# Two-layer transformer kernel: where the attention's folded maxima are transposed and added within a round

## The reference

```
b, n, c = x.shape                      # 8, 256, 128
qkv = x @ qkv_w.T + qkv_b              # 16 heads of 8 columns
attn = softmax(einsum('bhqd,bhkd->bhqk', q, k) / sqrt(8))
out = einsum('bhqk,bhkd->bhqd', attn, v)
return out @ proj_w.T + proj_b
```

## Time and profile before

| what | value |
|---|---|
| executions | 856.55, 856.58, 864.62 us; median 856.58 us |
| profiled execution | 864.53 us, of which the span from first to last instruction is 862.7 us |
| busy over the span | PE 689.3 us (80%), PEld 540.5 us (63%), DVE 673.7 us (78%), ACT 492.5 us (57%), POOL 128.6 us (15%) |
| granted TensorE clock over the span | mean 0.854 of full speed |
| rounds 0 and 1 of the attention | 24.35 and 20.79 us, clock 0.62 and 0.70 |
| rounds 2 and 3 | 18.80 and 18.77 us, clock 1.00 |
| rounds 4, 5, 6 | 20.45, 20.37, 21.37 us, clock 0.92, 0.92, 0.87 |
| round 7 | 23.14 us, clock 0.65 |
| round 8 | 20.46 us, clock 0.58 |

### The profile page before, as it was taken

One profiled execution on the slowest core, in us unless ns is written; L12 is line 12 of the kernel. 1 busy time (PEld: TensorE's weight loads), 2 busy tenths in 40 slices (PEclk: granted clock), 3 DMA queues, 4 the chain that ended last, 5 costly groups with the idle time before them and its releaser, 6 DMA issues. The chain is left out here.

```text
span 862.7 us, 14707 instructions
## 1 busy us (share of the span) xinstructions
PE 689.3 (80%) x5386; PEld 540.5 (63%) x5386; DVE 673.7 (78%) x1432; ACT 492.5 (57%) x893; POOL 128.6 (15%) x101
## 2 busy tenths in 40 slices
PE   6365765764669879999999867877877889999996
PEld 5254665664557657787778644444444458888886
DVE  3999899999975797989979848788775337777765
ACT  4667577778465566766867633666654543333232
POOL 1112113133304670010000047000000000000000
PEclk9578787777786998999989965899887579999999
DMA  7453343444415301103012040000000000000000
GB/s 230 99 143 111 105 117 99 101 126 121 132 41 179 98 25 55 44 1 99 1 34 66 0 147 0 2 1 2 1 2 1 1 1 1 1 13 1 13 13 13
DMA packets 76699, 48.30 MB, mean 56 GB/s; under 512 B 54994, under 2 KB 64980, under 8 KB 76628
## 3 DMA queue, kind: packets, MB, share of 16 engines
q1 hardware_dynamic: 73268, 44.75, 17.9%
q10 hardware_dynamic: 3360, 2.62, 1.0%
HBM read 37.85 MB, written 9.50 MB: 55 GB/s over the span
## 5 line engine op out<-in xcount | busy, mean ns | idle before, releaser
L983 ACT ACTIVATE hT<-hps,b1s 128x512 f32<-128x512 f32 x128 | 88.0, 691 | 67.3 <-PE hps L897 64.5
L1148 DVE TENSOR_TENSOR hl<-hT,hh 128x512 fp32r<-128x512 f32 x128 | 96.8, 777 | 28.7 <-ACT hh L989 27.2
L1592 DVE TENSOR_REDUCE mx<-s_ps 128x2 f32<-128x512 f32 x128 | 82.5, 687 | 42.0 <-PE s_ps L1351 41.6
L1525 ACT ACTIVATE pt<-st_ps 128x512 f32<-128x512 f32 x128 | 69.7, 600 | 48.4 <-PE st_ps L1361 48.3
L1820 ACT ACTIVATE act_h<-up 128x512 f32<-128x512 f32 x64 | 38.2, 598 | 87.7 <-PE up L1774 87.7
L320 ACT ACTIVATE rest<-rest,par 128x264 f32<-128x264 f32 x128 | 53.7, 502 | 36.7 <-DVE rest L591 36.7
L313 ACT ACTIVATE tap<-cst_s,par 128x328 f32<-128x328 f32 x128 | 72.4, 653 | 3.8 <-DVE par L644 3.8
L1902 DVE TENSOR_TENSOR hid<-act_h,up 128x512 f32<-128x512 f32 x64 | 43.3, 685 | 26.5 <-ACT act_h L1820 13.3
L1785 PEld LDWEIGHTS eo<-wc,hid 128*128 128x128 f32 x512 | 61.7, 192 | 2.4
L1785 PE MATMUL eo<-wc,hid 128*128 128x128 f32 x512 | 62.1, 275 | 0.0
L897 PE MATMUL hps<-xnh,w1h 128*128 128x512 f32 x128 | 55.9, 437 | 5.2 <-POOL w2l L805 4.5
(11 more groups left out here) (340 smaller groups left out, 1699.5 us busy)
## 6 DMA issues: line engine op xcount, KB each, us to landing
kd<-kst SPq DMA_DIRECT2D x16, 512.0 KB, 2.6
xc<-in_x_coarse SPq DMA_DIRECT2D x16, 512.0 KB, 4.2
wdB<-wdd SPq DMA_DIRECT2D x32, 256.0 KB, 5.2
dW<-kd SPq DMA_DIRECT2D x16, 256.0 KB, 3.3
Ks<-kd SPq DMA_DIRECT2D x64, 33.0 KB, 2.1
dW<-kd SPq DMA_DIRECT2D x64, 32.0 KB, 2.1
w1r<-in_w ACTq DMA_DIRECT2D x5, 256.0 KB, 2.9
w2r<-in_w ACTq DMA_DIRECT2D x5, 256.0 KB, 3.4
```

What stands on the lines that cost most here:

```text
L983: nc.scalar.activation(hT[k][:], hps[:, k, :], ACT.Gelu, bias=b1s[:, m:m + 1]).then_inc(h_done, 1)
L1148: nc.vector.tensor_tensor(hl[s % 2][:, k, :], hT[k][:], hh[s % 2][:, k, :].bitcast(F32), ALU.subtract).then_inc(hl_done, 1)
L1525: nc.scalar.activation(pt[h % 8][:].rearrange("p t q -> p (t q)"), st_ps[k][:], ACT.Exp, scale=SCALE)\
L1592: nc.vector.tensor_reduce(mx[:, :, h:h + 1], s_ps[k][:].rearrange("p (t k) -> p t k", t=2), AX, ALU.max).then_inc(s_used, 1)
```

## The change

The order of calls is changed in two places on TensorE and in one on VectorE. No instruction is added or taken away, and no wait is added: each `maxima` takes the waits along that stood before it.

```
@@ TensorE, round i @@
                     project(4 * i + 6)
+                if i - 1 in whole:
+                    pe.wait_ge(proj_used, min(4 * i + 6, PROJ))
+                    maxima(i - 1, 1, 2)
                 scores(i, 1)
...
                 values(i - 1, 0)
-                if i - 1 in whole:
-                    pe.wait_ge(proj_used, min(4 * i + 6, PROJ))
-                    maxima(i - 1, 1, 2)
                 scores(i, 3)
...
                     project(4 * i + 8)
+                scores(i, 5)
+                values(i - 1, 1)
                 if i in whole:
                     if i >= 2:
                         pe.wait_ge(o_ready, 2 * (i - 2) + 1)
                     else:
                         pe.wait_ge(proj_used, 4 * i + 7)
                     maxima(i, 0, 0)
-                scores(i, 5)
-                values(i - 1, 1)
@@ VectorE, round i @@
                 split(4 * i + 6)
+                add_maxima(i - 1, 1, 2)
                 largest(i, 2)
                 split(4 * i + 7)
                 largest(i, 3)
-                add_maxima(i - 1, 1, 2)
```

## The result

The changed kernel takes 851.79 us (median of 12 executions, 848.00 to 854.83) against 859.93 us of the kernel before (12 executions, 854.36 to 864.62). The ratio is 0.9887, with a 95% interval of 0.9862 to 0.9911: about 1.1% faster. The quotient of the two medians alone is 0.9905, so the gain is about 1% by either. The three executions that stood before the prediction had a median of 856.58; with twelve it is 3.4 us higher. The profiled execution of the changed kernel is one of its fastest, 848.22 us, where that of before, 864.53 us, lay above eleven of the twelve, so the two traces lie 16.3 us apart and the medians 8.1 us. The stages are therefore compared round by round.

The account below looks back on a forecast made before the run. In the attention, VectorE's reductions between scores were taken to bound each step at 1.9 us. From the median of 856.58 us, 2.95 for the order and 1.1 for the clock came off: 852.5 us, range 846.5 to 861.

Parts of the forecast that it names:

- The cycle of scores and reductions: Attention rounds: scores start only after VectorE reduced the step before, so a step costs 1.9 us at the least.
- Step 1 and the transposes' price: Round 3: four transposes now stand between a projection and these scores, cost 0.62 us and delay them that much.
- Steps 3 and 4: Round 3: the earlier addition delays the former by 0.88 us; the latter loses its stall but comes 0.10 us later.
- Step 5: Round 3: these scores, no longer behind the transposes and the wait for `averaged`, come 1.06 us earlier.
- Step 6: Round 3: TensorE's own work, 2.69 us with the transposes, sets these scores; the round is 0.45 us shorter.
- The sum at an unchanged clock: Attention stage: 2.25 us less in rounds 2 to 6, with rounds 0, 1 and 7 2.95 us less.
- The clock: Rounds 4 to 6: falls of the granted clock become rarer, worth 4.4 us, of which 1.1 count against the median.
- the third rival: Whole kernel: the clock gives all of its loss back, 849.2 us or 846; chance 0.15.
- The rule on transposes: TensorE: the skill says transposes do not count as work for the full clock, which speaks against the change.
- The rival that rested on it: Rounds 2 to 6: the clock falls more often, about 1.64 us each, 861.8 us in all; chance 0.12.
- the one that nothing is gained: Whole kernel: handoffs from VectorE are the long ones, or round 1 loses; 856.6 us, chance 0.15.
- the one of the full 17.4 us: Attention: both stalls go, 9.3 and 8.1 us, and nothing takes their place; 839.2 us, chance 0.05.

Follow-up runs that it names:

- e5: Changed kernel with the transposes of a batch's first half done twice into the same bank; 849.27 us, ratio 0.9885 to the kernel before.
- e6: Changed kernel with the second half's transposes directly behind a round's first scores, their addition between the first two steps' reductions; 851.03 us, ratio 0.9900.
- e1: Kernel before with only the first half's move, transposes and addition of the maxima earlier; 860.11 us against 860.17, ratio 0.9967.
- e11: Kernel before, order kept, with the repeated work of e3 and the unread matmuls of e9; 848.10 us, ratio 0.9867.
- e9: Changed kernel with added matmuls whose result nobody reads in rounds 6 to 8; 839.43 us, ratio 0.9735 to the kernel before.
- e2: Kernel before with only the second half's move, transposes behind the scores of Step 5 and its values; 852.99 us against 860.17, ratio 0.9923.
- e4: Changed kernel with the addition of the maxima back in its late place, the transposes staying early; 857.03 us, ratio 0.9949 to the kernel before.
- e0: The changed kernel itself, measured again; 849.35 us against 862.06 of the kernel before, ratio 0.9857.
- e3: Kernel before, order kept, with some transposes and projection matmuls done twice inside the two stalls; 856.15 us against 860.17, ratio 0.9952.
- e7: Changed kernel with the transposes of a batch's first half moved behind the scores of Step 6; 845.24 us, ratio 0.9825 to the kernel before.

## Why the prediction was right in the time and short in the size

The time, 852.5 us, was met to 0.7 us, and the range held. The size was not: I forecast 4.1 us less than a median of 856.58, and the medians of twelve lie 8.1 us apart. By the ratio it was faster by 1.1%, and to more than 1% I gave 0.15; by the medians it was 0.95%. That the number fits is luck: the gain was forecast 4.1 us too small, and the median of the three executions of before lay 3.4 us too low, and the two errors nearly cancel.

**The cycle of scores and reductions: right.** Steps that nothing else holds came after 1.92 and 1.85 us, where I had 1.88 and 1.87.

**Step 1 and the transposes' price: too high.** I took 0.62 us for four transposes, from the distance of starts before and behind them. Inserted in unbroken work behind a projection or behind the values they cost 0.44 (step 0 to 1: 2.77 against 2.33; e5: 2.91 against 2.47); directly behind step 0 they cost 0.59 (e6), so the price depends on the neighbours. The old distances, as I read it, held some time that the neighbours take anyway. I used the price twice in a round, and it makes 0.38 of the 0.43 us by which a round beat the forecast.

**Steps 3 and 4: right.** The addition was moved from one overflowing gap to another; e1 shows 0.09 us gained instead of 1.12, where I had 0.10 lost, and the price of the transposes (0.62 for 0.44) makes nearly all of that difference. One of my signs is badly put: what comes later by the addition is the pair of step 2 and then step 3. Step 2 itself came 0.37 later than before (4.70 us behind step 0 instead of 4.33), by the transposes.

**Step 5: right.** 1.85 us against the forecast 1.87.

**Step 6: right in kind.** TensorE's own work sets it (e5); measured 2.48 where I had 2.69.

**The sum at an unchanged clock: the step that was off.** Forecast 2.95 us, measured 7.1 between e11 and e9, of which 6.3 in rounds 2 to 7 at the full clock in both. The terms: rounds 2 to 6 2.25 against 4.4; round 7 0.5 against 1.85; the end of the stage 0 against 0.73; round 1 0.9 against 0.43, at clocks that differ; round 0 a loss of 0.7 against 0.36. In rounds 2 to 6 it is nearly all the price of the transposes, used twice (0.38 of 0.43 us). In round 7 I had priced them at the low clock, at which it ran before. At the full clock and without `project(4i+6)` the round has room for both groups of transposes: steps 0 to 4 take 7.72 us in e9 and 8.51 in e11, steps 4 to 6 3.89 and 4.96.

**The clock: right in direction, uncertain in size.** Falls in rounds 2 to 5 are gone in both profiles of the changed kernel. All profiled executions with a stall left as it was (before, e1, e2, e4) have such a fall, and none of the ten others does (changed, e0, e3 and e5 to e11). With e3, which keeps the order and only fills the stalls, this makes the idle time the cause. Not every stall is followed by a fall (rounds 2 and 3 of before), and what decides stays open. Of the 14.5 us between the two profiled stages, 7.1 are the order by e11 and e9, and the other 7.4, as what is left over, are put down to the clock. Of the 8.1 us between the medians I counted 1.1 for it, and 8.1 - 7.1 leaves 1.0; but no run measures that share, and the scatter of the executions is larger than it. I had put the 7.95 us between the profiled execution and the median down to fallen rounds; the runs show another place for such a scatter, the 505.3 to 511.7 us ahead of the attention. In size the 8.1 us are nearest to the third rival's 7.35, but that one had 2.95 for the order and 4.4 for the clock, and the order alone gives 7.1.

**The rule on transposes.** The Trainium skill (TensorE: Matmul & The Clock Gate, Part 4 on transposes), as the prediction reads it, would have the clock fall around step 3, where 0.90 us of idle time, one step, eight transposes and 0.40 us of idle time follow each other. It did not in any of rounds 2 to 5 of the changed kernel, in either profile. No run has transposes alone, so more than this the case doesn't show of the rule. The rival that rested on it falls. So do the one that nothing is gained and the one of the full 17.4 us, since the medians lie 8.1 us apart.

## What to carry to other kernels

A stall that the profile shows is worth only what the next bound leaves of it: here a stall of 1.12 us was worth 0.1 us in one place, where the addition behind it only moved to another full gap of VectorE, and one of 1.05 us was worth 0.8 in the other, where the transposes went to a place at which VectorE had already freed their bank. Look for the place where the engine is idle while it waits for something else (e7), and read the queue of the third engine before moving work off the second (e6). In this kernel TensorE's idle time also cost clock: matmuls that nobody reads made this kernel faster by about as much as the whole change did.

## What the runs showed that was not expected

Adding nine matmuls of 512 columns in each of rounds 7 and 8, and six in round 6, took the kernel from 0.9857 (0.9887 in the first comparison) to 0.9735 of the time before, about 10 us or more, by holding the granted clock at 1.00 from round 2 to the end of the stage. And the time ahead of the attention differs by up to 6.4 us between the profiled executions, which have the same instructions there, 505.3 to 511.7 us; I did not look into why. It is as large as most of what was tested here.
